# Three heads of P instead of two turned by VectorE and transfers, in eight units of an attention stage

## The chip, the cores and the metric

The kernel runs on one core of a Trainium2 chip. The metric is the device time of one execution in microseconds, from launch to end; three runs are shown by their median. The engines are TensorE (PE, with its weight loads as PEld), VectorE (DVE), ScalarE (ACT), GpSimd (POOL) and SyncE (SP), which here issues all DMA transfers.

## The reference

Two layers of a gated cross-attention model over x, 16 sequences of 128 tokens with 512 features each, in float32. The change lies in the attention of the second layer. For each sequence and each of its 16 heads of width 32:

```python
qh = (layernorm(x) @ Wq.T)    # 16 heads of 32
k, v = split(ctx @ Wkv_expand.T, 2)
scores = where(causal, qh @ kh.T / sqrt(32), lowest)
P = softmax(scores)           # 128 x 128 for a head and a sequence
x = x + tanh(g) * ((P @ vh) @ Wout.T)
```

Before it come a latent attention and an expert network, after it a last network with a softmax over eight experts.

## The kernel before

The 16 sequences are handled four at a time, so a tile is 128 partitions by 4 x 128 columns. The attention stage has 16 units: unit u is group m = u // 4 of four sequences and group g = u % 4 of four heads, so a unit has four heads j, and for each head a 128 x 512 tile of P (four sequences side by side). Each engine runs its own written-out list of instructions and waits on semaphores; the order within a list is fixed by hand.

The loop runs over steps u = 0 to 17. In step u:

- TensorE computes the scores of unit u - 1 (`scores3`, 32 small matmuls into banks 4 to 7, one for each head), Q and K of unit u (`q3`, `k3`), the attention output of unit u - 3 (`av3`), at g = 2 the four V blocks of the group (`v3`), in some steps one or two output blocks (`wo3`), transposes of P of unit u - 2 (`turn3`), and transposes of normed tiles (`ln_turn`). All but the scores take their PSUM bank from `ring3`, four banks in turn; a take waits until the bank's earlier content has been read.
- VectorE takes the largest value of each score row (`largest`, four reductions), turns P of unit u - 2 (`turn_p3`), copies Q out of PSUM (`q3_out`), takes reciprocals of the sums (`inverse`), writes masks into score banks (`seed3`), computes the low half of the attention output (`av3`), copies K and two V blocks (`k3`, `v3`), adds the output blocks to the residual (`final3`) and treats the normed tiles.
- ScalarE computes the exponentials of unit u - 1 (`exp3`, four for each head), the high half of the attention output, two V copies, the remaining seeds, and copies TensorE's transposes of P from PSUM into PT3 (`turn3`). In steps 8, 9, 12 and 13 the seeds are followed by the P copies; in steps 11, 14 and 15 the P copies come last, behind the splits of the normed tiles. Steps 7 to 9, 11 to 13 and 15 have seeds; after the others TensorE writes the mask itself.
- GpSimd multiplies P by the reciprocals (`norm3`) and splits weights.
- SyncE stores and loads the turned heads (`p3_store`, `p3_load`), then loads normed tiles, context, weights and X tiles in a fixed order.

`av3` needs P transposed within each sequence, since the keys must lie on the partitions. There are two ways. Heads 2 and 3 are transposed by TensorE against the identity, four 128 x 128 transposes for each head, and copied by ScalarE into `PT3`. Heads 0 and 1 are turned by VectorE in 32 x 32 blocks (`turn`, `blocks_in`, `blocks_out`) into `P3Y`; one transfer stores P3Y to the scratch `pscr` in device memory, and four transfers load it back into `PTV` with the blocks exchanged among the partitions. Store and load of unit u - 2 are issued in step u and used by `av3` in step u + 1. The store waits for the last turn; the loads wait for the store's landing and for the attention output of unit u - 3, which still reads the place. `exp3` of unit u waits until head j of unit u - 2 has been turned, as it writes the same half of `P3`.

Of the kernel before, what the change touches and what calls it, by code (L numbers as in the profile page):

```python
# [10 lines left out]
F32 = mybir.dt.float32  # L11
# [169 lines left out]
def build(nc, i, out):  # L181
    ctx = ExitStack()
    with ctx:
# [10 lines left out]
        def sb(name, shape, dt, st=None):  # L194
            return (st or ctx).enter_context(nc.sbuf_tensor(name, shape, dt))

        on_pe, on_act, on_dve, on_pool = (sig(n) for n in ("on_pe", "on_act", "on_dve", "on_pool"))
        ps = Psum(on_pe, [ctx.enter_context(nc.psum_tensor(f"bank{k}", [128, 512], F32)) for k in range(8)])
# [6 lines left out]
        STG = sb("STG", [128, 3456], F32)  # L205
# [52 lines left out]
        P3 = sb("P3", [128, 2, 2048], F32)  # L258
        PTV = sb("PTV", [128, 4096], F32)
        XF = sb("XF", [128, 4, 512], F32)  # L260
        sm3 = sb("sm3", [128, 2, 4, 8], F32)

        def ar(o, n):
            return AR[:, o:o + n]
# [32 lines left out]
                   O=(ar(2304 + 2304 * g, 512), ar(2816 + 2304 * g, 512))) for g in range(4)]  # L297
        PT3 = PTV[:, 0:2048]

        P3Y, P3Z = STG[:, 2048:3072], PTV[:, 0:1024].rearrange("p (j n c) -> p n j c", j=4, n=8)  # L300
        Q3, K3 = MSK[:, 0, :], MSK[:, 1, :]
        V3 = PTV[:, 2048:4096].rearrange("p (b n) -> p b n", b=4)
        OT2 = [ar(o, 4096).rearrange("p (h g n) -> p h g n", h=2, g=4) for o in (14336, 28672)]
# [15 lines left out]
        vscr = [nc.dram_tensor(f"vscr{k}", [128, 512], F32, kind="Internal").ap() for k in range(2)]  # L319
        l4scr = [nc.dram_tensor(f"l4scr{k}", [128, 512], F32, kind="Internal").ap() for k in range(4)]  # L320
        pscr = [nc.dram_tensor(f"pscr{k}", [128, 1024], F32, kind="Internal").ap() for k in range(2)]
        xs = [i["x"], scr[0], scr[1], scr[2], out]

        def rows(ph, m, tb):
# [34 lines left out]
        t_p3, d_p3 = sig("t_p3", 16), sig("d_p3", 16)  # L359

        def kinds(count, names):
            return [Part(count, n) for n in names.split()]
# [7 lines left out]
        p3y_ok, cx_ok = kinds(on_dve, "p3y_ok cx_ok")  # L370
# [85 lines left out]
        def blocks_in(t):  # L456
            return t.rearrange("p (n i c) -> p n i c", i=4, c=32)

        def blocks_out(t):
            return t.rearrange("p (i n c) -> p n i c", i=4, c=32)  # L460
# [34 lines left out]
        n, f = 0, 0  # L495
        for u in range(27, 35):
            k = 0
# [24 lines left out]
        pc_step, n = {}, 0  # L522
# [24 lines left out]
        def seeded(u):  # L547
            return 7 <= u < 16 and u % 4 != 2


        def k_first(u):
            return 3 <= u < 8
# [19 lines left out]
        def tensor(pe):  # L572
# [265 lines left out]
            for u in range(NU + 3):  # L838
                m, p = divmod(u, 8)
# [49 lines left out]
            for F in range(NF):  # L889
                m, f = divmod(F, 16)  # L890
# [82 lines left out]
                            ins.then_inc(*ps.fill(("s3", u, j)))  # L973

            def turn3(u, ring):
                for b in (2, 3):
                    k = ps.take(("pt3", u, b), ring.next())
                    pe.wait_ge(*ps.free(("pt3", u, b)))
                    pe.wait_ge(*nm3_ok[u, b])
                    for n in range(4):  # L980
                        s = slice(512 * b + 128 * n, 512 * b + 128 * n + 128)
                        ins = pe.transpose(k[:, 128 * n:128 * n + 128], P3[:, u % 2, s], ident[:, :])
                    ins.then_inc(*ps.fill(("pt3", u, b)))

            def av3(u, ring):
                m, g = divmod(u, 4)
                k = ps.take(("av", u), ring.next())
                pe.wait_ge(*ps.free(("av", u)))
                for b in range(4):
                    pe.wait_ge(*ps.drained(("v3", m, b)))  # L990
                pe.wait_ge(*d_p3[u, 3])
                pe.wait_ge(*ps.drained(("pt3", u, 2)))
                pe.wait_ge(*ps.drained(("pt3", u, 3)))
                for b in range(4):
                    for j in range(4):
                        h = 4 * g + j
                        o = k[32 * j:32 * j + 32, 128 * b:128 * b + 128]
                        if j < 2:
                            ins = pe.matmul(o.rearrange("p (a c) -> p a c", a=4), V3[:, b, 32 * h:32 * h + 32],
                                            P3Z[:, 4 * j + b], True, True)  # L1000
                        else:
                            ins = pe.matmul(o, V3[:, b, 32 * h:32 * h + 32],
                                            PT3[:, 512 * j + 128 * b:512 * j + 128 * b + 128], True, True)
                ins.then_inc(*ps.fill(("av", u)))
# [135 lines left out]
        def scalar(ac):  # L1140
# [151 lines left out]
            for u in range(NU + 3):  # L1292
                m, p = divmod(u, 8)
# [72 lines left out]
            for F in range(NF):  # L1366
                m, f = divmod(F, 16)
# [37 lines left out]
            def exp3(u, js):  # L1405
                for j in js:
                    S, k = sm3[:, u % 2, j, :], ps.ap(("s3", u, j))
                    ac.wait_ge(*nb_ok["3", u, j])
                    if u >= 2:
                        ac.wait_ge(*(p3y_ok[u - 2, j] if j < 2 else ps.full(("pt3", u - 2, j))))  # L1410
                    for b in range(4):
                        c = 512 * j + 128 * b
                        ins = ac.act(P3[:, u % 2, c:c + 128], k[:, 128 * b:128 * b + 128], ACT.Exp, bias=S[:, b:b + 1],
                                     scale=1.0, accum_out=S[:, 4 + b:5 + b])
                    ins.then_inc(*(ex_ok.mark(("3", u, j)) if seeded(u + 1) else ps.drain(("s3", u, j), on_act)))
# [6 lines left out]
            def turn3(u, b):  # L1422
                ac.wait_ge(*ps.full(("pt3", u, b)))
                if u:
                    ac.wait_ge(*ps.full(("av", u - 1)))
                ac.act(PT3[:, 512 * b:512 * b + 512], ps.ap(("pt3", u, b))[:, :],
                       ACT.Copy).then_inc(*ps.drain(("pt3", u, b), on_act))
# [21 lines left out]
            for u in range(18):  # L1449
                m, g = divmod(u, 4)  # L1450
                values = u > 4 and g == 2
                if 1 <= u <= 16:
                    exp3(u - 1, (0, 1))
                if u >= 3 and not k_first(u):
                    av3(u - 3)
                if values and not k_first(u):
                    v3(m, 1)
                if 1 <= u <= 16:
                    exp3(u - 1, (2,))
                if values and not k_first(u):  # L1460
                    v3(m, 3)
                if u in (3, 5, 6):
                    av3(u - 3)
                if u in ():
                    for tb in tiles3(u)[g - 1]:
                        ln_turn(*after3(m), tb)
                if 1 <= u <= 16:
                    exp3(u - 1, (3,))
                if k_first(u) and u not in (3, 5, 6):
                    av3(u - 3)  # L1470
                if values and k_first(u):
                    v3(m, 1)
                    v3(m, 3)
                if seeded(u):
                    for j in range(len(by_vector(u)), 4):
                        seed3(u, j)
                if u >= 2 and u not in (3,7,11,14,15):
                    turn3(u - 2, 2)
                    turn3(u - 2, 3)
                if u >= 16:  # L1480
                    h4(0, (0, 1) if u == 16 else (2, 3))
                if u < 16 and g:
                    for tb in tiles3(u)[g - 1]:
                        ln_turn(*after3(m), tb)
                if u < 16 and g == 3 and m + 1 < NM:
                    cx_split(m + 1)
                if u in (3,7,11,14,15):
                    turn3(u - 2, 2)
                    turn3(u - 2, 3)
            av3(15)  # L1490

            def logits(m):
# [42 lines left out]
        def vector(ve_):  # L1535
            e = ve_
# [209 lines left out]
            for u in range(NU + 3):  # L1746
                m, p = divmod(u, 8)
# [122 lines left out]
            for F in range(NF):  # L1870
                m, f = divmod(F, 16)
# [69 lines left out]
                e.recip(S[:, 4:8], S[:, 4:8]).then_inc(*rc_ok.mark(("3", u, j)))  # L1941

            def turn_p3(u):
                for j in range(2):
                    e.wait_ge(*nm3_ok[u, j])
                    if u:
                        e.wait_ge(*t_p3[u - 1])
                    e.turn(blocks_out(P3Y)[:, 4 * j:4 * j + 4],
                           blocks_in(P3[:, u % 2, 0:1024])[:, 4 * j:4 * j + 4]).then_inc(*p3y_ok.mark((u, j)))

            def av3(u):
                m, g = divmod(u, 4)
# [348 lines left out]
        def sync(e):  # L2301
# [120 lines left out]
            for u in range(NU + 3):  # L2422
                m, p = divmod(u, 8)
# [51 lines left out]
            for F in range(NF):  # L2475
                m, f = divmod(F, 16)
# [56 lines left out]
                e.dma(rows(3, m, tb), XF[:, tb, :]).then_inc(*t_xf[tb].mark(m))  # L2533

            def p3_store(u):
                e.wait_ge(*p3y_ok[u, 1])
                if u >= 2:
                    e.wait_ge(*d_p3[u - 2, 3])
                e.dma(pscr[u % 2], P3Y).then_inc(*t_p3.mark(u))

            def p3_load(u):
                e.wait_ge(*t_p3[u])
                if u:
                    e.wait_ge(*ps.full(("av", u - 1)))
                src = pscr[u % 2].rearrange("(j r) (i x) -> i r j x", j=4, i=4)
                for k in range(4):
                    e.dma(PTV[32 * k:32 * k + 32, 0:1024].rearrange("r (j x) -> r j x", j=4), src[k]).then_inc(*d_p3.mark((u, k)))

            for u in range(18):
                m, g = divmod(u, 4)  # L2550
# [65 lines left out]
            for m in range(NM):  # L2616
# [9 lines left out]
                if more:  # L2626
# [8 lines left out]
                    if m:  # L2635
                        for tb in range(4):
                            n = 4 * ((m - 1) % 2) + tb
# [117 lines left out]
```

## Time and profile before

| | us |
|---|---|
| median of 3 runs | 1331.37 |
| lowest, highest | 1330.41, 1332.07 |
| the profiled execution | 1332.48 |
| its span, first to last instruction | 1330.7 |
| TensorE busy | 1311.2 (99%) |
| VectorE busy | 942.3 (71%) |
| ScalarE busy | 517.6 (39%) |
| GpSimd busy | 405.7 (30%) |

The granted clock of TensorE is at its full level, 2.4 GHz (1.00 in the profile), in all of the span. Busy shares are averages over the whole span; the stage of the change fills about 1011 to 1190 us of it. In the rows below an instruction is given by its engine, the line of the kernel (mostly of a helper: L118 a matmul, L121 a transpose by TensorE, L124 a ScalarE activation, L164 a turn by VectorE, L170 a transfer), its output and inputs, and their shapes. "idle before" is the time in which the engine stood still ahead of the instruction, with what released it.

### The profile page before, as it was taken

Reading aid. Unit: us, or ns where it says so; the run is one execution under the profiler, and the core shown is the slowest. Engines: PE = TensorE matmul, PEld = TensorE weight load, DVE = VectorE, ACT = ScalarE, POOL = GpSimd, SP = SyncE. Lnnn points to the kernel's source line nnn. Section 1 sums busy time; section 2 is a strip of 40 time slices with the busy share of each in tenths; the row PEclk is TensorE's granted clock in tenths of the full one; section 3 lists DMA queues with packets and bytes.
Section 4 is the critical chain, followed back from the end, with each engine's and each line's share of the span. In section 5 each row is a group of like instructions: output and inputs, shape, how many; then the busy total and the mean of one; then the engine's idle time right before and its main releaser. Section 6 shows DMA issues by size and latency. Waiting matters only on the chain.

```text
span 1330.7 us, 20251 instructions
## 1 busy us (share of the span) xinstructions
PE 1311.2 (99%) x7348; PEld 1063.7 (80%) x7348; DVE 942.3 (71%) x1813; ACT 517.6 (39%) x1569; POOL 405.7 (30%) x462
## 2 busy tenths in 40 slices
PE   7999999999999999999999999999999999999998
PEld 6788888888888788878887888788887777878887
DVE  5766676675785878785678668777888888846643
ACT  3545455455464321231114111321126888832220
POOL 4113322231255352201111112114435876630000
PEclk9999999999999999999999999999999999999999
DMA  8755454443573232210121112122333656465651
GB/s 302 229 161 166 156 168 136 159 157 119 190 217 91 80 87 86 84 44 17 46 90 32 52 40 80 52 63 65 103 100 130 215 179 210 159 205 175 214 166 56
DMA packets 136564, 168.97 MB, mean 127 GB/s; under 512 B 16145, under 2 KB 87953, under 8 KB 136465
## 3 DMA queue, kind: packets, MB, share of 16 engines
q1 hardware_dynamic: 136464, 167.68, 39.9%
q8 instruction: 58, 0.95, 0.3%
q14 instruction: 42, 0.34, 0.1%
HBM read 113.09 MB, written 54.53 MB: 126 GB/s over the span
## 4 chain that ended last, share of the span: by engine, by line
PE 90%; DVE 4%; ACT 3%; DMA 1%; issue 1%; POOL 0%; SPq 0%; DVEq 0%; ACTq 0%; POOLq 0%
PE bank L118 88%; PE bank L121 2%; ACT P L124 2%; DVE STG L130 1%; DVE AH L130 1%; DVE XR L140 1%; ACT STG L124 0%; DVE AH L127 0%; DMA PTV<-pscr 0%; DMA XR<-in_x_dram 0%; DVE sm L146 0%; ACT AR L124 0%; DMA pscr<-STG 0%; DMA STG<-in_WqT_dram 0%; SPq L170 0%
## 5 line engine op out<-in xcount | busy, mean ns | idle before, releaser
L118 PE MATMUL bank<-XT,AR 128*128 128x512 f32 x1152 | 279.7, 392 | 0.1
L118 PE MATMUL bank<-AR 128*128 128x512 f32 x1056 | 257.4, 395 | 0.1
L118 PEld LDWEIGHTS bank<-XT,AR 128*128 128x128 f32 x1152 | 214.2, 188 | 47.0 <-ACT STG L124 0.5
L124 ACT ACTIVATE STG<-bank,b1c 128x512 f32<-128x512 f32 x128 | 88.3, 690 | 384.8 <-PE bank L118 292.1
L118 PEld LDWEIGHTS bank<-AR 128*128 128x128 f32 x1056 | 194.6, 188 | 47.7 <-issue 3.3
L118 PE MATMUL bank<-AR,CT 128*128 128x512 f32 x768 | 191.3, 392 | 0.0
L118 PE MATMUL bank<-AR,AH 128*128 128x512 f32 x768 | 185.4, 390 | 0.0
L118 PEld LDWEIGHTS bank<-AR,AH 128*128 128x128 f32 x768 | 143.9, 188 | 30.1 <-DVE AH L130 0.4
L127 DVE CAST AH<-STG 128x512 fp32r<-128x512 f32 x192 | 94.3, 491 | 103.1 <-PE bank L118 91.4
L118 PEld LDWEIGHTS bank<-AR,CT 128*128 128x128 f32 x768 | 140.2, 188 | 26.9
L127 POOL CAST BA<-STG 128x256 fp32r<-128x256 f32 x64 | 32.8, 512 | 390.1 <-PE bank L118 242.1
L130 DVE TENSOR_TENSOR AH<-STG,AH 128x512 fp32r<-128x512 f32 x192 | 141.4, 737 | 6.6
L124 ACT ACTIVATE Pb<-bank,sm 128x128 f32<-128x128 f32 x256 | 89.9, 377 | 90.9 <-DVE sm L136 90.9
L130 POOL TENSOR_TENSOR Pb<-Pb,sm 128x512 f32<-128x512 f32 x64 | 66.6, 1043 | 148.1 <-DVE sm L149 145.6
L118 PE MATMUL bank<-TM,BA 128*128 128x512 f32 x384 | 107.4, 391 | 2.3 <-DVE TM L130 1.4
L124 ACT ACTIVATE P<-bank,sm 128x128 f32<-128x128 f32 x256 | 90.0, 391 | 23.6 <-DVE sm L146 23.6
L118 PE MATMUL bank<-AH,BA 128*128 128x512 f32 x384 | 97.4, 389 | 0.0
L130 DVE TENSOR_TENSOR STG<-STG 128x512 f32<-128x512 f32 x128 | 90.3, 705 | 4.2
L130 DVE TENSOR_TENSOR CT<-bank,CT 128x512 fp32r<-128x512 f32 x64 | 44.1, 688 | 66.0 <-ACT CT L124 65.9
L130 POOL TENSOR_TENSOR rstd<-ve,mhalf 128x1 f32<-128x1 f32 x64 | 38.5, 603 | 169.9 <-DVE ve L136 169.9
L118 PEld LDWEIGHTS bank<-TM,BA 128*128 128x128 f32 x384 | 71.5, 188 | 20.0 <-issue 2.5
L118 PEld LDWEIGHTS bank<-AH,BA 128*128 128x128 f32 x384 | 72.1, 188 | 15.3
(145 smaller groups left out, 1803.7 us busy)
## 6 DMA issues: line engine op xcount, KB each, us to landing
XR<-scr SPq DMA_DIRECT2D x68, 256.0 KB, 2.9
pscr<-PYZ SPq DMA_DIRECT2D x30, 512.0 KB, 2.9
PYZ<-pscr SPq DMA_DIRECT2D x120, 128.0 KB, 3.0
XR<-in_x_dram SPq DMA_DIRECT2D x32, 256.0 KB, 3.9
XR<-lscr SPq DMA_DIRECT2D x128, 64.0 KB, 2.0
scr<-XR SPq DMA_DIRECT2D x32, 256.0 KB, 2.1
pscr<-STG SPq DMA_DIRECT2D x16, 512.0 KB, 2.6
PTV<-pscr SPq DMA_DIRECT2D x64, 128.0 KB, 2.8
```

The costliest lines, as they stand in the source:

```text
L118: return self.e.matmul(o, w, x, start=start, stop=stop, skip_group_check=True) if self.e else Nothing()
L121: return self.e.transpose(o, x, ident) if self.e else Nothing()
L124: return self.e.activation(o, x, func, **kw) if self.e else Nothing()
L127: return self.e.tensor_copy(o, x) if self.e else Nothing()
L130: return self.e.tensor_tensor(out=o, in0=a, in1=b, op=op) if self.e else Nothing()
L140: return self.e.scalar_tensor_tensor(out=o, in0=a, scalar=s, in1=b, op0=op0, op1=op1) if self.e else Nothing()
```

## The change

In units 6 to 13 (function `turned3`), thus in steps 8 to 15, head 2 goes the way of heads 0 and 1: VectorE turns three heads, one store carries 128 x 1536 elements instead of 128 x 1024, and the four loads bring 192 KB each instead of 128 KB. TensorE transposes and ScalarE copies head 3 alone. The turned heads get a tile of their own (`P3S`) instead of a part of `STG`, and a scratch of their own size (`p3scr`). All other units keep two heads. Since TensorE takes one bank less of the ring in each of those steps, the banks of what follows are other ones.

```diff
+        P3S = sb("P3S", [128, 1536], F32)
...
-        P3Y, P3Z = STG[:, 2048:3072], PTV[:, 0:1024].rearrange("p (j n c) -> p n j c", j=4, n=8)
+        P3Y = [P3S[:, 0:512 * k] for k in range(4)]
+        P3Z = [PTV[:, 0:512 * k].rearrange("p (j n c) -> p n j c", j=4, n=4 * k) if k else None for k in range(4)]
...
+        p3scr = [nc.dram_tensor(f"p3scr{k}", [128, 1536], F32, kind="Internal").ap() for k in range(2)]
...
+        def turned3(u):
+            return 3 if 6 <= u < 14 else 2
...
             def turn3(u, ring):
-                for b in (2, 3):
+                for b in range(turned3(u), 4):
...
-                pe.wait_ge(*ps.drained(("pt3", u, 2)))
-                pe.wait_ge(*ps.drained(("pt3", u, 3)))
+                for b in range(turned3(u), 4):
+                    pe.wait_ge(*ps.drained(("pt3", u, b)))
...
-                        if j < 2:
+                        if j < turned3(u):
...
-                                            P3Z[:, 4 * j + b], True, True)
+                                            P3Z[turned3(u)][:, 4 * j + b], True, True)
...
-                        ac.wait_ge(*(p3y_ok[u - 2, j] if j < 2 else ps.full(("pt3", u - 2, j))))
+                        ac.wait_ge(*(p3y_ok[u - 2, j] if j < turned3(u - 2) else ps.full(("pt3", u - 2, j))))
...
-                    turn3(u - 2, 2)
-                    turn3(u - 2, 3)
+                    for b in range(turned3(u - 2), 4):
+                        turn3(u - 2, b)
...
             def turn_p3(u):
-                for j in range(2):
+                n = turned3(u)
+                for j in range(n):
...
-                    e.turn(blocks_out(P3Y)[:, 4 * j:4 * j + 4],
-                           blocks_in(P3[:, u % 2, 0:1024])[:, 4 * j:4 * j + 4]).then_inc(*p3y_ok.mark((u, j)))
+                    e.turn(blocks_out(P3Y[n])[:, 4 * j:4 * j + 4],
+                           blocks_in(P3[:, u % 2, 0:512 * n])[:, 4 * j:4 * j + 4]).then_inc(*p3y_ok.mark((u, j)))
...
             def p3_store(u):
-                e.wait_ge(*p3y_ok[u, 1])
+                n = turned3(u)
+                e.wait_ge(*p3y_ok[u, n - 1])
...
-                e.dma(pscr[u % 2], P3Y).then_inc(*t_p3.mark(u))
+                e.dma(p3scr[u % 2][:, 0:512 * n], P3Y[n]).then_inc(*t_p3.mark(u))
...
-                src = pscr[u % 2].rearrange("(j r) (i x) -> i r j x", j=4, i=4)
+                src = p3scr[u % 2][:, 0:512 * n].rearrange("(j r) (i x) -> i r j x", j=4, i=4)
                 for k in range(4):
-                    e.dma(PTV[32 * k:32 * k + 32, 0:1024].rearrange("r (j x) -> r j x", j=4), src[k]).then_inc(*d_p3.mark((u, k)))
+                    e.dma(PTV[32 * k:32 * k + 32, 0:512 * n].rearrange("r (j x) -> r j x", j=4), src[k]).then_inc(*d_p3.mark((u, k)))
```

## Rows read from the trace of the kernel before

**Rows 1.** Stretches: length; PE, PEld, DVE, ACT, POOL busy; clock; DMA share; GB/s.
```profile
1093.20:1103.60 10.40, 10.36 (x107) 8.57 (x108) 9.61 (x24) 8.38 (x37) 8.65 (x9) 1.00 0.63 197
1114.60:1127.10 12.50, 12.39 (x114) 9.94 (x113) 9.50 (x19) 9.58 (x40) 3.87 (x4) 1.00 0.65 196
```

**Rows 2.** Waits of TensorE, 1060 to 1190 us: us in all, times, longest.
```profile
PE bank L118 <- ACT bank L124: 0.4, 2, 0.2
```

**Rows 3.** ScalarE in order of time: start, us, what, steps 9, 11, 15.
```profile
1088.19 0.60 ACT L124 ACTIVATE AR<-bank 128x512 fp32r<-128x512 f32 x1 [0.35 <-PE bank L118]
1091.42 1.68 ACT L124 ACTIVATE bank<-mkb 128x512 f32<-128x512 bf16 x3
1113.31 1.22 ACT L124 ACTIVATE bank<-mkb 128x512 f32<-128x512 bf16 x2
1157.09 1.17 ACT L124 ACTIVATE bank<-mkb 128x512 f32<-128x512 bf16 x2
```

**Rows 4.** TensorE in order of time, steps 10 to 12.
```profile
1093.24 1.17 PE L118 MATMUL bank<-MSK 32*128 32x128 f32 x32 [0.18 <-ACT bank L124]
1097.30 1.08 PE L118 MATMUL bank<-PTV 128*32 128x128 f32 x32
1101.89 1.04 PE L121 MATMUL bank<-ident,P 128*128 128x128 f32 x8
1102.76 1.04 PE L121 MATMUL bank<-ident,XR 128*128 128x128 f32 x8
1108.62 1.08 PE L118 MATMUL bank<-PTV 128*32 128x128 f32 x32
1118.85 1.08 PE L118 MATMUL bank<-PTV 128*32 128x128 f32 x32
```

**Rows 5.** Instructions grouped by line and shape, 1070 to 1160 us.
```profile
L124 ACT ACTIVATE PTV<-bank 128x512 f32<-128x512 f32 x22 | 12.5, 634 | 5.9 <-PE bank L121 4.7 <-PE bank L118 1.2
L164 DVE STREAM_TRANSPOSE STG<-P 128x512 f32<-128x512 f32 x16 | 10.4, 688 | 0.0
```

**Rows 6.** VectorE in order of time, steps 10 and 11.
```profile
1097.68 1.30 DVE L164 STREAM_TRANSPOSE STG<-P 128x512 f32<-128x512 f32 x2
1098.90 0.66 DVE L136 TENSOR_SCALAR MSK<-bank 128x512 f32<-128x512 f32 x1
1099.61 0.67 DVE L130 TENSOR_TENSOR AR<-bank,AR 128x512 fp32r<-128x512 f32 x1
1105.36 1.29 DVE L130 TENSOR_TENSOR AR<-bank,AR 128x512 fp32r<-128x512 f32 x2 [1.51 <-ACT AR L124]
```

**Rows 7.** DMA issues of the whole span: count, size, median us to landing.
```profile
XR<-lscr SPq DMA_DIRECT2D x128, 64.0 KB, 2.0
scr<-XR SPq DMA_DIRECT2D x32, 256.0 KB, 2.1
pscr<-STG SPq DMA_DIRECT2D x16, 512.0 KB, 2.6
PTV<-pscr SPq DMA_DIRECT2D x64, 128.0 KB, 2.8
```

**Rows 8.** TensorE from 1099.80 us: the third V block of step 10.
```profile
1099.80 0.40 PE L118 MATMUL bank<-AR 128*128 128x512 f32 x1
```

**Rows 9.** SyncE's queue in order of time, steps 9 and 11.
```profile
1092.33 1.74 SPq L170 DMA_DIRECT2D PTV<-pscr  x4
1112.97 1.74 SPq L170 DMA_DIRECT2D PTV<-pscr  x4
```

**Rows 10.** Landing: the store of step 9, the loads of steps 9 to 11.
```profile
DMA to landing us min/median/max: 4.4/4.4/4.4
DMA to landing us min/median/max: 2.7/2.9/3.1
DMA to landing us min/median/max: 2.6/2.8/4.4
DMA to landing us min/median/max: 2.6/2.8/3.5
```

More of the change, by code:

```diff
@@ L1487, in scalar @@
                 if u in (3,7,11,14,15):
-                    turn3(u - 2, 2)
-                    turn3(u - 2, 3)
+                    for b in range(turned3(u - 2), 4):
+                        turn3(u - 2, b)
             av3(15)
@@ L2535, in p3_store @@
             def p3_store(u):
-                e.wait_ge(*p3y_ok[u, 1])
+                n = turned3(u)
+                e.wait_ge(*p3y_ok[u, n - 1])
                 if u >= 2:
                     e.wait_ge(*d_p3[u - 2, 3])
-                e.dma(pscr[u % 2], P3Y).then_inc(*t_p3.mark(u))
+                e.dma(p3scr[u % 2][:, 0:512 * n], P3Y[n]).then_inc(*t_p3.mark(u))
             def p3_load(u):
+                n = turned3(u)
                 e.wait_ge(*t_p3[u])
```

## The prediction

> **What bounds the kernel.** The page first: TensorE is busy for 99% of the span. So a change is worth what it takes out of TensorE's queue, less what newly holds that queue. Then the loop of the attention stage: its steps 8 to 15, which the change touches, lie between 1070.7 and 1158.7 us (a step is reckoned from its 32 score matmuls to those of the next). In the table of stretches [rows 1] TensorE has no room; VectorE is free for 0.8 us in step 10 and 3.0 us in step 12, ScalarE for 2.0 and 2.9. Third, TensorE's waits [rows 2]: 0.4 us in two, both on ScalarE's seeds of the score banks. ScalarE's timeline [rows 3] shows the place: in step 9 it writes three masks until 1093.10, and the scores follow at 1093.24 after an idle 0.18 us [rows 4]; step 13 repeats that. In steps 11 and 15 the seeds end at 1114.53 and 1158.26, shortly before the scores at 1114.68 and 1158.66: ScalarE is the second bound there. In steps 8 and 12, with two output blocks each, TensorE alone decides.
>
> **Removed.** TensorE's transposes of head 2. The eight transposes of two heads take 1102.76 - 1101.89 = 0.87 us [rows 4], so the four give back 0.44 us; over eight units 3.5 us is the ceiling. ScalarE loses one 128x512 copy into PTV, 634 ns by itself and 0.48 us of pitch [rows 5].
>
> **Added.** VectorE turns a third head: 688 ns by itself, at a pitch of (1098.90 - 1097.68)/2 = 0.61 us [rows 5, 6]. The attention matmuls read another operand through strides; all 32, of plain and of strided heads, take 1.08 us [rows 4], so I cost that at nothing. SyncE issues as many transfers as before, five per unit, but each is half as large again. The store: 256 KB of another tile land in 2.1 us and these 512 KB in 2.6 [rows 7], so the third 256 KB cost 0.5. The four loads grow from 128 to 192 KB each. Four 64 KB loads of the normed tiles land in 2.0 us and these in 2.8, so one more 64 KB costs 0.8 at most; at least 0.3, a little over half of what the store pays for the same 256 KB, since the rest hides between the issues. I take 0.5. The turned P then arrives 0.6 + 0.5 + 0.5 = 1.6 us later after the start of its turn, between 1.4 and 1.9.
>
> **TensorE's 0.44 us, step by step.**
> Steps 8 and 12: TensorE decides, so it is saved. VectorE's reductions of the next step follow the last output block, which doesn't move against the step's start, so ScalarE's first exponentials gain next to nothing; they have some 0.35 us to spare ahead of the attention output, and I count 0.42 each: 0.84.
> Steps 9 and 13: the seeds hold the next scores and hang on the exponentials behind the attention output, none of which starts earlier. TensorE idles 0.62 us instead of 0.18: 0 each.
> Step 10: here VectorE's extra 0.61 us meets TensorE. The third V block takes the PSUM bank of this step's Q (the ring has four banks, and Q stands four takes before it). VectorE copies Q out right after the turns, until 1098.90 + 0.66 = 1099.56 [rows 6]; TensorE starts that block at 1099.80 [rows 8]. With a third turn ahead of it the copy ends at 1100.17, and TensorE waits 0.4 us. The fourth V block waits in the same way for the low half of the attention output (1099.61 + 0.67 = 1100.28 becomes 1100.89): another 0.05. So 0.45 is lost where 0.44 is saved: 0. ScalarE, however, comes to its splits of the normed tiles 0.48 us earlier, and VectorE, which idles 1.51 us for these [rows 6], to the reductions of step 11.
> Step 11: these let the exponentials start earlier, and the seeds end 0.35 to 0.4 earlier, as the attention output itself comes when it did. TensorE's own 0.44 is there: 0.40.
> Step 14 is step 10 again: 0. ScalarE does those splits ahead of its P copies there, so nothing comes of its shorter list.
> Step 15: TensorE is ready 0.44 earlier, the seeds are over at 1158.26, some 0.05 for the signal: 0.35.
> Together 0.84 + 0.40 + 0.35 = 1.6 us.
>
> **The turned heads come later.** The attention matmuls of a step wait for the last of the four loads of the step before, issued 1.31 us after the first. Step 9: first load 1092.33 [rows 9], last 1093.64, landing 3.1 later [rows 10], at 1096.7; the matmuls start at 1097.30 [rows 4]: 0.55 us to spare. But its store took 4.4 us where the median is 2.6; with 2.6 there would be 2.3 to spare. Step 10: last load 1102.94 + 4.4 = 1107.3, matmuls at 1108.62: 1.3 to spare, or 2.8 if the load took the usual 2.9. Step 11: first load 1112.97, last 1114.29 + 3.5 = 1117.8, matmuls at 1118.85: 1.05 to spare. Every other step has more than 2. In step 11 the turn starts 0.48 us earlier and the matmuls are due 0.40 earlier, so the data is late by 1.6 - 1.05 - 0.08, about 0.5 us, and step 12, which TensorE bounds, pays it. The slow store of step 9 and the slow load of step 10 I take for chance that need not come again; they are priced in the second rival. What is queued behind the five transfers on SyncE (normed tiles, a weight block, X tiles) is issued about 1 us later; it is read a step later or off TensorE's path, and I cost it at nothing, 1 us if one of them was just in time. GpSimd gets nothing to do.
>
> **Sum.** 1.6 - 0.5 = 1.1 us. The profiled execution took 1332.48 us with a span of 1330.7, about 1.1 above the median of 1331.37. Its span should be 1329.6, the median 1330.3. A measurement of this kernel tells 0.2%, 2.7 us, from no change: the forecast is no measurable change.
>
> **The cases.**
> *As forecast* (0.50): 1330.3, its own range 1329.3 to 1331.3.
> *The transfers eat it all* (0.24): the slow landings come again. Step 9's data is late by 1.6 - 0.55 = 1.05 us, of which 0.45 is the wait for VectorE anyway, step 10's by 0.3: 1.1 - 0.6 - 0.3 = 0.2 us, 1331.2. For it: three of the landings of steps 9 to 11 are slow [rows 10]. Against: the medians are 2.6 and 2.8.
> *VectorE becomes the bound* (0.06): it would use 0.6 of its 0.8 free us in step 10, and each late copy moves the next step. Against: 3.0 us free in step 12. If steps 10, 11, 14 and 15 lost 0.3 more each: 1331.5.
> *Slower* (0.09): the turned heads come L later, and L is more than I sized. Steps 9 to 11 then lose 3L - 2.9 us together, others a little from L = 2.3 on. Slower by 2.7 needs 1.6 + 2.7 = 4.3 us of lateness, so L = 2.4, half as much again as my sum. At L = 2.7 it is 5.2 and some 0.4 elsewhere, 4.0 slower: 1335.4. For it: landings of 4.4 us occur, and the DMA share of these steps is past 0.6 [rows 1]. Against: L would have to be so large in three successive steps.
> The Trainium skill (DMA: Bandwidth & Descriptors, Latency and other measured facts) puts an access to device memory at 0.2 us on average and 2 us at high load, and calls it the main part of a transfer's fixed cost. By that rule L could be 1.6 + 1.8 = 3.4, an estimate, and the kernel some 8 us slower; the landings of 2.6 to 4.4 us here show such a spread, but not in every step.
> *Faster beyond doubt* (0.09): the bank waits of steps 10 and 14 stay out, the transfers are in time, and the seeds don't hold steps 9 and 13: near the ceiling, 1331.4 - 3.2 = 1328.2. Against: the rows above on every count.
> *Nothing changes* (0.02): 1331.4; hardly, with four transposes less per unit in the fullest queue.
>
> Faster by over 0.2%: the fifth case and a sliver of the first, 0.10. Slower: 0.09. Within: 0.81. The range leaves out some 1.5 in 10, the outer parts of those two: 1328.4 to 1333.2.
>
> **What would show it.** TensorE: 32 transposes of P fewer; waits on VectorE of about 0.4 us ahead of the third V block in steps 10 and 14; idle ahead of the scores that follow steps 9 and 13 grown from 0.18 to 0.6 us; a wait of 0.5 us on the load into PTV in step 12. VectorE: three turns in a row at 1.83 us of pitch. The store lands in 3.1 us, the loads in 3.1 to 3.4. From step 16 on all is as before, 1.1 us earlier. The prediction is wrong if step 9 or 13 gets shorter, if step 10 shows no wait on VectorE, or if more than one step waits for PTV.

## The result: slower by a third of a percent

| | before | changed |
|---|---|---|
| median of 8 runs, us | 1331.23 | 1335.66 |
| lowest, highest | 1330.21, 1332.07 | 1333.87, 1338.85 |
| ratio, 95% interval | | 1.0033, 1.0024 to 1.0042 |
| profiled execution, its span | 1332.48, 1330.7 | 1335.13, 1333.3 |

The change costs 4.4 us in the median where I had forecast a gain of 1.1 (the profiled execution, 0.5 below the median, costs 2.6 against the profiled one of before). The time lies outside the stated range (up to 1333.2) and close to the rival called *Slower*, which had 1335.4 and a chance of 0.09.

TensorE's waits in the trace of the changed kernel, 1000 to 1200 us (us in all, times, longest); the view of before held one line for the later part of it [rows 2]:

```profile
PE bank L118 <- DVE P3S L164: 2.8, 2, 2.0
PE bank L118 <- DMA PTV<-p3scr: 2.0, 1, 2.0
PE bank L118 <- DVE st L152: 1.5, 2, 0.7
...
PE bank L118 <- ACT bank L124: 0.3, 1, 0.3
```

TensorE in order of time, where it stands still (start, length, instruction, idle before it):

```profile
1091.71 1.17 PE L118 MATMUL bank<-MSK 32*128 32x128 f32 x32 [0.74 <-DVE st L152]
...
1097.86 1.08 PE L118 MATMUL bank<-PTV 128*32 128x128 f32 x32 [2.02 <-DVE P3S L164]
...
1114.74 1.17 PE L118 MATMUL bank<-MSK 32*128 32x128 f32 x32 [0.28 <-ACT bank L124]
...
1120.93 1.08 PE L118 MATMUL bank<-PTV 128*32 128x128 f32 x32 [2.00 <-DMA PTV<-p3scr]
...
1143.88 1.08 PE L118 MATMUL bank<-PTV 128*32 128x128 f32 x32 [0.68 <-DVE sm L146]
...
1155.71 1.08 PE L118 MATMUL bank<-PTV 128*32 128x128 f32 x32 [0.74 <-DVE P3S L164]
```

The attention matmuls of steps 10 and 12 wait 2.0 us each, those of steps 14 and 15 another 0.7 each; before, none of the four waited, they followed the Q matmuls directly (steps 10 to 12 in [rows 4]). Three of the four waits are put down to VectorE. But the turns that VectorE makes at the time of the first are those of the next unit, which these matmuls don't read:

```profile
1095.99 1.88 DVE L164 STREAM_TRANSPOSE P3S<-P 128x512 f32<-128x512 f32 x3
```

Read the transfers instead. These are SyncE's issues of step 9, and the time to landing of the store and of each of the four loads, in order:

```profile
1087.20 0.32 SPq L170 DMA_DIRECT2D p3scr<-P3S  x1
1090.45 1.74 SPq L170 DMA_DIRECT2D PTV<-p3scr  x4
```

```profile
DMA to landing us min/median/max: 3.2/3.2/3.2
DMA to landing us min/median/max: 3.2/3.2/3.2
DMA to landing us min/median/max: 3.6/3.6/3.6
DMA to landing us min/median/max: 4.1/4.1/4.1
DMA to landing us min/median/max: 6.0/6.0/6.0
```

The last load was issued at 1091.8 and landed 6.0 later, at 1097.8: 0.1 us ahead of the matmuls. In steps 12, 14 and 15 too the matmuls start within 0.1 us of the landing of the last load. Before, the last load of this step landed in 3.1 us [rows 10]. In step 11 it took 5.2 us (3.5 before), in the other six changed steps 4.0 to 4.8 (2.9 to 3.1 before, but for step 10: 4.4 before, 4.0 now). Over the span the two kinds of transfer, in the view of the DMA issues:

```profile
p3scr<-P3S SPq DMA_DIRECT2D x8, 768.0 KB, 3.4
PTV<-p3scr SPq DMA_DIRECT2D x32, 192.0 KB, 3.6
```

Against 2.6 and 2.8 [rows 7]. Last, the steps as stretches, from scores to scores (length; busy time of PE, PEld, DVE, ACT, POOL; clock; DMA share; GB/s):

```profile
1069.51:1081.36 11.85, 11.85 (x108) 9.46 (x108) 9.72 (x19) 8.63 (x38) 5.80 (x6) 1.00 0.58 185
1081.36:1091.71 10.35, 9.61 (x100) 7.67 (x100) 9.71 (x23) 8.68 (x38) 9.14 (x9) 1.00 0.76 240
1091.71:1104.82 13.11, 11.09 (x107) 8.47 (x108) 10.45 (x25) 8.52 (x39) 11.39 (x11) 1.00 0.78 228
1104.82:1114.74 9.92, 9.64 (x101) 7.68 (x100) 9.29 (x19) 8.39 (x39) 5.80 (x6) 1.00 0.74 256
1114.74:1128.72 13.98, 11.96 (x107) 9.46 (x107) 9.84 (x20) 8.73 (x38) 4.13 (x4) 1.00 0.81 224
1128.72:1139.10 10.38, 9.64 (x100) 7.67 (x100) 9.71 (x23) 8.68 (x38) 7.32 (x7) 1.00 0.63 212
1139.10:1150.84 11.74, 11.06 (x108) 8.47 (x108) 10.35 (x25) 8.52 (x39) 9.71 (x9) 1.00 0.66 200
1150.84:1161.35 10.51, 9.71 (x100) 7.69 (x100) 9.45 (x19) 8.49 (x39) 5.69 (x5) 1.00 0.84 253
```

The same steps of before, by the starts of TensorE's score matmuls: 12.30, 10.22, 11.35, 10.09, 12.41, 10.23, 11.34 and 10.00 us, 87.9 in all; here they are 91.8, so 3.9 longer. (The span grew by 2.6 only, because the profiled execution of before came to step 8 1.2 us later than that of the changed kernel: it had waited for turned heads in step 6, which the change doesn't touch.) Steps 8 and 11 gain 0.4 and 0.2, steps 10 and 12 lose 1.8 and 1.6, steps 14 and 15 0.4 and 0.5. The DMA share of these steps was 0.50 to 0.67 before and is 0.58 to 0.84 here. What follows step 15 takes as long as before, to 0.1 us.

### The profile page after: what moved, and what is told of

The parts are those of the page before. It is cut to its first block, busy times and chain, and to the rows that moved or that the text cites. A ratio compares the mean times of both kernels' runs of the same rounds, so it can differ in the third digit from the quotient of the medians.

```text
span 1333.3 us, 20172 instructions
## 1 busy us (share of the span) xinstructions
PE 1307.6 (98%) x7316; PEld 1060.1 (80%) x7316; DVE 945.8 (71%) x1821; ACT 514.4 (39%) x1561; POOL 405.8 (30%) x462
## 4 chain that ended last, share of the span: by engine, by line
PE 90%; DVE 4%; ACT 3%; DMA 1%; issue 1%; POOL 0%; SPq 0%; DVEq 0%; ACTq 0%; POOLq 0%
PE bank L118 88%; ACT P L124 2%; PE bank L121 2%; DVE sm L146 1%; DVE st L152 0%; DMA PTV<-p3scr 0%; DVE STG L130 0%; DVE AR L130 0%; DMA XR<-in_x_dram 0%; DVE P3S L164 0%; ACT PTV L124 0%; SPq L170 0%; ACT AR L124 0%; DMA STG<-in_WqT_dram 0%; DMA p3scr<-P3S 0%
```

## The experiments

Each was timed against the kernel before on the same chip. Its medians there were 1331.35, 1331.13 and 1331.39 us for the three sets of four.

| run | median, us | ratio, 95% interval |
|---|---|---|
| e1_tiles_only | 1331.45 | 0.9998, 0.9989 to 1.0007 |
| e2_two_sent | 1329.83 | 0.9985, 0.9976 to 0.9994 |
| e3_third_turn | 1332.55 | 1.0006, 0.9997 to 1.0015 |
| e4_bytes_only | 1339.19 | 1.0054, 1.0040 to 1.0068 |
| e5_bytes_clean | 1334.87 | 1.0029, 1.0017 to 1.0040 |
| e6_padded | 1341.45 | 1.0073, 1.0059 to 1.0087 |
| e7_three_units | 1329.55 | 0.9988, 0.9979 to 0.9997 |
| e8_two_units | 1337.33 | 1.0050, 1.0036 to 1.0063 |
| e9_head_apart | 1332.70 | 1.0008, 0.9999 to 1.0017 |
| e10_apart_from_0 | 1339.07 | 1.0058, 1.0044 to 1.0071 |
| e11_apart_two_units | 1331.96 | 1.0007, 0.9997 to 1.0016 |
| e12_small_pieces | 1339.08 | 1.0057, 1.0042 to 1.0072 |

### The change taken apart

**e1_tiles_only.**

```diff
         def turned3(u):
-            return 3 if 6 <= u < 14 else 2
+            return 2
```

> The changed kernel with two turned heads in all units: only the new tile, the new scratch and its row pitch of 6144 B are left of the change. Theory (late transfers of three heads cost the time): 0.0 us against before, within 0.1%. Rival A (the tile, the scratch or its pitch cost it): 4 us slower. Rival B (the runs with a lower granted clock belong to the layout): the same spread of 5 us as the changed kernel.

0.1 us from before, well inside the interval: the tile, the scratch and its pitch cost nothing that shows. The runs spread over 2.5 us, all at a granted clock of 1.000, so the spread of 5 us doesn't come with the layout either.

**e2_two_sent.**

```diff
-                e.dma(p3scr[u % 2][:, 0:512 * n], P3Y[n]).then_inc(*t_p3.mark(u))
+                e.dma(p3scr[u % 2][:, 0:1024], P3Y[2]).then_inc(*t_p3.mark(u))
...
             def p3_load(u):
-                n = turned3(u)
+                n = 2
```

(Head 2 is turned into a third of P3S of its own, and read from its old place in PTV.)

> The changed kernel, but the store and the four loads carry only the first two heads, as before; VectorE still turns three, TensorE still transposes one. It leaves out the transfer of head 2, whose old content is read. Theory: with landings as before (last load about 3.0 us) only the 0.6 us of the third turn comes on top, no wait of 2 us on the turned heads is left, and the saving of 1.1 to 1.6 us shows: 1329.6 to 1330.2, and no spread of 5 us. Rival C (VectorE's third turn costs the time): 4 us slower, as with the full transfers.

1.5 us faster, and no run above 1330.96. TensorE in order of time:

```profile
1090.88 1.18 PE L118 MATMUL bank<-MSK 32*128 32x128 f32 x32 [0.74 <-DVE st L152]
...
1094.97 1.08 PE L118 MATMUL bank<-PTV 128*32 128x128 f32 x32
1095.98 4.08 PE L118 MATMUL bank<-AR 128*128 128x512 f32 x15
```

The attention matmuls wait for nothing. The 15 matmuls of V and K behind them take 4.08 us, where the kernel before took 3.74 for them: here, where no transfer hides it, is the wait for VectorE's copies, 0.34 us (0.42 in step 14). Its eight steps are 11.86, 10.34, 11.28, 9.69, 11.91, 10.36, 11.30 and 9.70 us, against before -0.44, +0.12, -0.07, -0.40, -0.50, +0.13, -0.04 and -0.30: in all -1.5.

**e3_third_turn.**

```diff
             def turn_p3(u):
-                for j in range(2):
+                for j in range(3 if 6 <= u < 14 else 2):
```

(The third turn goes to a spare tile; the store and ScalarE's exponentials of head 2 wait for it.)

> The kernel before with one turn more on VectorE in the eight units (into a spare tile, read by nobody); TensorE, ScalarE and the transfers as before. Theory: nothing is saved, steps 10 and 14 wait 0.45 us each for VectorE's copies, the store is issued 0.6 us later, which step 10 may feel by up to 0.5: 0.9 to 1.4 us slower. Rival C: 4 to 6 us slower.

1.2 us slower, with an interval that just takes in no change. TensorE waits 0.24 us ahead of the third V block of step 10, and again in step 14:

```profile
1096.75 1.65 PE L118 MATMUL bank<-AR 128*128 128x512 f32 x6
1098.64 2.37 PE L118 MATMUL bank<-AR 128*128 128x512 f32 x9 [0.24 <-DVE MSK L136]
```

The 15 matmuls take 4.26 us from first to last here, 0.52 more than before. Steps 10 and 14 are 0.5 us longer each and the other six no longer than before, to 0.03 us; no attention matmul of the eight steps waits. So what the third turn costs is its place ahead of VectorE's copies in these two steps, and the store that is issued later costs nothing.

**e4_bytes_only and e5_bytes_clean.** The opposite: VectorE turns two heads, TensorE transposes and ScalarE copies two, and only the transfers are half as large again. ScalarE's copy of head 2 goes to a free part of STG, since the loads cover its old place.

```diff
-                for b in range(turned3(u), 4):
+                for b in (2, 3):
...
-                for j in range(n):
+                for j in range(2):
...
-                ac.act(PT3[:, 512 * b:512 * b + 512], ps.ap(("pt3", u, b))[:, :],
+                ac.act(pt_at(u, b), ps.ap(("pt3", u, b))[:, :],
```

> The kernel before with transfers half as large again in the eight units (a third head's place of zeros is stored and loaded, read by nobody); VectorE turns two heads, TensorE transposes two, ScalarE copies two. Theory: the data comes about 2.2 us later than before (store 0.6, last load 1.6) with nothing saved, steps 10 and 12 wait for it by 1.2 to 2 us each, others a little: 3 to 5 us slower. Rival C: 0.5 us at most.

7.8 us slower, more than expected. A part of it has a reason of its own: with a fill of the third place with zeros by GpSimd in step 1, TensorE waited 3.7 us in step 2, where the kernel before waits 1.0. The run was repeated without it:

> As e4_bytes_only, but without the filling of zeros that held step 2 for 3.7 us there (one early turn of VectorE fills the third place instead). Theory: the waits for the turned heads in steps 11 and 12 of e4_bytes_only (0.75 and 2.7 us) remain, and perhaps one in step 10, and the stretch of lower clock behind the longest: 3 to 5 us slower than before. Rival C (VectorE's third turn is the cost): within 0.5 us of before.

3.7 us slower, with one long wait among TensorE's waits, in step 12 (and 0.65 us in step 10):

```profile
PE bank L118 <- DMA PTV<-p3scr: 2.2, 1, 2.2
```

So the larger transfers alone, read by nobody, cost 3.7 us; the rest of the change alone gains 1.5. The two don't add up to the 4.4 of the whole, and needn't: in the changed kernel the same late loads meet a turn that ends 0.6 us later and matmuls that are due up to 0.4 us earlier, and so four steps wait and not two. How much of the 3.7 is the store and how much the loads, no run tells apart; the landings below do.

### Which units

**e7_three_units and e8_two_units.** `turned3` gives 3 for units 6, 10 and 13, and for units 7 and 9.

> The change in units 6, 10 and 13 alone (steps 8, 12 and 15), whose turned heads have 3.1 to 4.5 us to spare. Theory: the 2.8 us of delay fit in, no wait for the turned heads, TensorE's 0.44 us show in all three: 0.9 to 1.3 us faster than before. If other places lose by the change too: no gain.

> The change in units 7 and 9 alone (steps 9 and 11), whose turned heads have 0.55 to 1.05 us to spare (2.3 in step 9 with a quick store). Theory: both waits of 2 us of the changed kernel's profile are there, nearly all that the change costs: 2 to 4 us slower than before, with some runs at a lower granted clock and a wide spread. If the cost is spread over all units: about 1 us slower.

The three units with room (before, the last load of steps 8, 12 and 15 lands over 3 us ahead of its matmuls: in step 8 it is issued at 1079.68 + 1.31, lands some 2.9 later, and the matmuls start at 1087.04) gain 1.6 us, and this version beats both kernels (0.9988, interval below 1), though in its trace the last load of step 12 lands only 0.15 us ahead of its matmuls. The two without lose 6.2 us, more than all eight together, and more than expected. The sum 6.2 - 1.6 = 4.6 is close to the 4.4 of the whole, but don't lean on it: units 8, 11 and 12 are in neither run, and the wait of step 12 is 3.0 us here and 2.0 in the whole. The waits of the two, 1.6 in step 10 and 3.0 in step 12, in the view of TensorE's waits:

```profile
PE bank L118 <- DMA PTV<-p3scr: 3.0, 1, 3.0
PE bank L118 <- DVE P3S L164: 1.6, 1, 1.6
```

### What makes the loads slow

**e6_padded.** The pieces of a row begin 2048 B apart.

```diff
-                e.dma(p3scr[u % 2][:, 0:512 * n], P3Y[n]).then_inc(*t_p3.mark(u))
+                e.dma(p3scr[u % 2].rearrange("p (i x) -> p i x", i=4)[:, :, 0:128 * n],
+                      P3Y[n].rearrange("p (i x) -> p i x", i=4)).then_inc(*t_p3.mark(u))
```

> The changed kernel with a scratch whose four pieces of a row (1536 B each) begin 2048 B apart, not 1536 B; the store writes 512 pieces of 1536 B instead of 128 of 6144 B. Theory D (the loads are slow, 4.2 to 6.0 us for the last one, because pieces of 1536 B lie across boundaries of 2048 B in device memory): the last load lands in at most 3.6 us, the waits shrink to under 1 us, the kernel gains 2 to 4 us over the changed one. Theory E (it is the number of bytes, or what else is on the queues): the last load stays above 4.2 us and the time within 1 us of the changed kernel, or worse for the smaller pieces of the store.

5.8 us slower than the changed kernel. The last load takes 4.7 to 6.0 us, no less than there (4.0 to 6.0), and the store 3.8 to 5.6. Boundaries of 2048 B are not it.

**e12_small_pieces.** Three heads in one store and four loads, each head a block of 512 columns of its own.

```diff
-                src = p3scr[u % 2][:, 0:512 * n].rearrange("(j r) (i x) -> i r j x", j=4, i=4)
+                src = p3scr[u % 2].rearrange("(j r) (h i x) -> i r h j x", j=4, h=3, i=4)
```

> The changed kernel, one store and four loads of 192 KB as there, but the loads read and write pieces of 512 B (one head each) in place of 1536 B. Pieces of 512 B took 28 ns each in the trace and those of 1536 B 105, so if the size of a piece is the trouble: the last load lands in 3.6 to 4 us in place of 4.2 to 6, and the kernel gains 1 to 3 us over the changed one. If it is the number of bytes: within 1 us of the changed kernel.

The last load takes 4.0 to 5.8 us and the kernel is 3.4 us slower than the changed one. Small pieces don't help; the first load already takes 3.1 to 3.4 us. The loads are also issued 0.65 us apart here, not 0.43, so they ask for only 302 GB/s, what the 128 KB loads of before asked for, and still land about 1.0 us apart.

**e9_head_apart, e11_apart_two_units, e10_apart_from_0.** Head 2 has transfers of its own.

```diff
+                e.dma(p3scr[u % 2][:, 0:1024], P3Y[2]).then_inc(*t_p3.mark(u))
+                if n == 3:
+                    e.wait_ge(*p3y_ok[u, 2])
...
+                    e.dma(p3scr[u % 2][:, 1024:1536], P3S[:, 1024:1536]).then_inc(*t_p3b.mark(u))
...
+                if n == 3:
+                    e.wait_ge(*t_p3b[u])
...
+                        e.dma(PTV[32 * k:32 * k + 32, 1024:1536].rearrange("r (j x) -> r j x", j=4), src[k]).then_inc(*d_p3b.mark((u, k)))
```

> The changed kernel with head 2 sent apart: heads 0 and 1 are stored as soon as they are turned and loaded as before, head 2 has a store of 256 KB and four loads of 64 KB of its own, issued behind. Theory (the four loads of 192 KB, 0.43 us apart, ask for more than the queues move, so that each lands 0.45 us later than the one before): loads of 128 and 64 KB keep up with the issues, the last one lands 0.9 us later than before and not 2.8, nearly no wait for the turned heads is left, and the 1.5 us of the kernel that sent only two heads come back: 1329.5 to 1330.5. Rival (it is the bytes in any form, or the longer queue of SyncE): 3 us slower or more.

> As e8_two_units (units 7 and 9 alone, 6 us slower than before), but with head 2 sent apart. Theory: the two waits go, 0 to 1 us from before. Rival (the bytes in any form): 3 us slower or more.

> As e9_head_apart, but in units 0 to 13. Steps 2 to 7 are held by ScalarE and by the landing of the turned heads. If ScalarE's shorter list (0.48 us a step) counts more there: 1 to 2 us faster than e9_head_apart. If the landing does (step 6 already waited 1.2 us for it in the profile of before): 1 to 4 us slower.

With the two critical units this turns 6.2 us of loss into 0.6, so it is not the bytes in any form: loads of 128 and 64 KB land in 2.2 to 3.6 us. I had added the issues wrongly, though: the last of eight loads goes out 3.2 us after the first, not 1.3. From the first issue to the last landing there are 5.2 to 6.4 us in e9_head_apart, against 4.2 to 4.8 before (5.8 in step 10), so the data comes 1 to 2 us later and not 0.9. In all eight units a loss of 1.3 us is left (the interval just takes in none), and it has a new place. SyncE's issues of steps 10 and 11, then the landing of the store issued at 1108.51:

```profile
1100.05 3.65 SPq L170 DMA_DIRECT2D PTV<-p3scr  x8
1103.74 1.50 SPq L170 DMA_DIRECT2D XR<-in_ctxT_dram  x1
1105.28 0.43 SPq L170 DMA_DIRECT2D STG<-in_U_dram  x1
1106.05 1.75 SPq L170 DMA_DIRECT2D XF<-scr  x4
1108.51 0.91 SPq L170 DMA_DIRECT2D p3scr<-P3S  x2
```

```profile
DMA to landing us min/median/max: 5.7/5.7/5.7
```

What was queued behind the loads is now issued right ahead of the next store, which takes 5.7 us, and step 12 waits 2.4 us (step 14 another 0.9). That the one slows the other is read from their order; no run moved them apart. From unit 0 on it is worse (7.7 us slower): in the profiled execution, the slowest of five, the attention matmuls wait 1.1, 3.4 and 1.1 us in steps 4 to 6, 4.1 in step 8 and 2.4 in step 12, so the landings count there, not ScalarE's list.

## Why the prediction was wrong

The step that failed is the sum in **Added**: "The turned P then arrives 0.6 + 0.5 + 0.5 = 1.6 us later". Step 13, where no landing of before was slow, shows it: from the start of the turn to the landing of the last load there were 8.4 us before (1130.68 to 1139.07) and 11.1 after; step 11 gives 8.8 and 11.8, and the mean of the eight steps is 8.9 and 11.6. So the delay is 2.6 to 3.0 us. Of its three terms

- the turn, 0.61, was right (three turns take 1.88 us in a row, two took 1.30);
- the store, 0.5, was nearly right: 3.2 to 3.5 us in six of the eight steps against 2.6, and 3.9 and 4.5 in steps 12 and 14;
- the loads, 0.5, were mis-sized: the last one takes 4.8 us to land in the mean of the eight steps against 3.2 before, 1.5 more; by steps 1.3 to 1.9 more in six and 2.9 in step 9, and only step 10, slow before, has 0.4 less. I had added a cost to one load, and had the rest hide between the issues. But the four are issued 0.43 us apart, and at 192 KB each lands 0.4 to 0.5 us later after its issue than the one before (3.2, 3.6, 4.1 in step 9), so one is through every 0.87 us, 226 GB/s, while 452 are asked for. At 128 KB, 301 GB/s at the same spacing, the time to landing grew too, only little (2.7, 2.8, 2.9, 3.1): from 1092.33 + 2.7 to 1093.64 + 3.1 the four land 0.57 us apart, 229 GB/s. From the first to the third load, over all eight steps, it is 230 GB/s before and 207 after. So the queue moved the loads no faster before; it was already a little behind the issues, and nothing of the added bytes could hide. At 226 GB/s another 64 KB is 0.29 us for each of the four loads, 1.2 us together, an estimate from these landings; the rest of the 1.5 is in the slow last loads.

The other steps of the prediction, against e2_two_sent, which has the change without its bytes:

- The savings: +1.6 us forecast, 1.5 measured, and by steps 0.42, 0, 0, 0.40, 0.42, 0, 0, 0.35 forecast against 0.44, -0.12, 0.07, 0.40, 0.50, -0.13, 0.04, 0.30. That steps 9 and 13 give nothing back, because ScalarE's seeds hold the next scores, is right. They even lose 0.1 us: the seeds end as long after the start of the step as before (10.1 us in step 9), but the scores follow them after 0.25 us instead of 0.14. The trace shows one more semaphore instruction of TensorE's queue there, 0.11 us behind the other, that waits for VectorE; this accounts for the 0.1 us.
- The bank wait of steps 10 and 14: 0.45 forecast; the matmuls behind it take 0.34 and 0.42 longer there, and 0.5 in e3_third_turn. In the changed kernel it can't be seen, as the forecast of the second case had it: the longer wait for the data covers it.
- Which steps wait: step 12 (0.5 forecast, 2.0 measured) and, not forecast, steps 10 (2.0), 14 and 15 (0.7 each). The prediction had named more than one such step as a sign that it was wrong. I took the slow store of step 9 for chance; it was, the store took 3.2 us this time, but then the loads took its place. The slow last load of step 10 (4.4 us) was not mere chance: with two heads on the way it comes again in e1_tiles_only, e3_third_turn and e7_three_units (4.2 to 4.6), though not in e2_two_sent and e8_two_units (2.8 and 3.3).
- The rival *Slower* had the mechanism right, and its L of 2.7. That its 1335.4 came within 0.3 us of the median is partly luck: it has steps 9 to 11 late, and only two of these three made TensorE wait, while two later steps waited 0.7 each and a part of the median goes with a lower clock (below). I gave it 0.09 because "L would have to be so large in three successive steps"; but what makes L large is no accident of a step: from the first to the third they land 0.9 to 1.1 us apart in all eight. The estimate from the Trainium skill (DMA: Bandwidth & Descriptors, Latency and other measured facts), which the prediction set beside that rival, had L at 3.4 and 8 us; the runs show 2.6 to 3.0 and 4.4.
- *VectorE becomes the bound* is refuted as the main cause: e3_third_turn, with the third turn alone, loses 1.2 us. The tile and scratch have no part (e1_tiles_only).

Open: what sets the rate of these loads. The size of the pieces and their boundaries don't (e12_small_pieces, e6_padded). And why the last load of a step takes 4.0 to 6.0 us. It is worst in steps 9 and 11, in e8_two_units and e12_small_pieces as well (5.6 to 6.0), but in steps 10 and 11 in e5_bytes_clean; other transfers are issued directly behind it in all eight steps, so their being there doesn't explain it, and no run moved them away.

## What to carry to other kernels

When a transfer grows, don't price it by its own landing alone: divide the bytes by the spacing of the issues and set that beside the rate at which such loads land in the trace of before, from landing to landing. If they already land further apart than they are issued (0.57 against 0.43 us here), each added byte comes on top. Then see what lies right behind them. And reckon the slack of the consumer in each iteration: the same change gains 1.6 us in the three units with over 3 us of room and loses 6.2 us in the two with 0.55 and 1.05. A slow landing in one trace may be chance or may come back: of the two here one did, as other versions of the kernel show.

## What the hardware showed besides

Some long waits cost TensorE more than their length. In e12_small_pieces it stands still for 3.63 us in step 12, and what follows runs slowly:

```profile
1122.07 1.93 PE L118 MATMUL bank<-PTV 128*32 128x128 f32 x32 [3.63 <-DMA PTV<-p3scr]
1123.93 8.19 PE L118 MATMUL bank<-AR 128*128 128x512 f32 x27
```

The same two groups take 1.08 and 6.42 us in the changed kernel. The table of stretches shows the granted clock there (it stands third from the end of a line, ahead of the DMA share):

```profile
1110.00:1120.00 10.00, 8.15 (x66) 6.34 (x64) 9.65 (x20) 8.54 (x38) 4.26 (x5) 1.00 0.64 193
1120.00:1130.00 10.00, 7.93 (x51) 6.25 (x52) 4.04 (x9) 4.40 (x19) 2.04 (x2) 0.66 0.65 203
```

A mean of 0.66 between the levels 1.0 (2.4 GHz) and 0.5 (1.2 GHz) means that 6.8 of the 10 us (0.34 / 0.5) were at the lower one, partly while idle, and 2.6 us were lost in those two groups beyond the wait. In e4_bytes_only the clock falls likewise after an idle time of 2.68 us (a mean of 0.83 from 1120 to 1130 us). But in the profiled execution of e8_two_units it stays at full level after a wait of 3.0 us, so the length of the wait alone doesn't decide. The changed kernel's waits of 2.0 us left it at full level in the profiled execution, but three of its eight timed runs have a mean granted clock of 0.997 to 0.999, and these are the three slowest, 1337.6 to 1338.9 us; the other five, at 1.000, lie between 1333.9 and 1336.2. The median without them would be 1334.2, so about 1.5 us of the loss go with the clock. In e8_two_units the runs at a lower clock are no slower than the others (1337.2 to 1337.7 against 1337.0 to 1337.7), so the link is not a strict one, and no run here separates it.
